# Attention inner loop on one Trainium2 core: one row-tiled stretch a step, and weighted sums over 512 columns one step behind

## What is computed

```python
scores = jnp.einsum('bqhd,bkhd->bhqk', Q, K) / np.sqrt(HEAD_DIM).astype(np.float32)
slopes = 0.5 ** jnp.arange(NUM_HEADS, dtype=jnp.float32)
rel = pos[None, :] - pos[:, None]
scores = scores + slopes[None, :, None, None] * rel[None, None, :, :]
attn = jax.nn.softmax(scores, axis=-1)
out = jnp.einsum('bhqk,bkhd->bqhd', attn, V)
```

## Time and profile before

| what | value |
|---|---|
| median of 3 runs | 5108.2 us (5095.89 to 5113.9) |
| span of the profiled execution | 5138.9 us (its own device time isn't listed) |
| TensorE busy / weight loads | 4706.1 us (92%) / 2589.8 us (50%) |
| VectorE, ScalarE busy | 4275.5 us (83%), 3471.8 us (68%) |
| GpSimd busy | 1377.0 us (27%) |
| mean granted TensorE clock | 0.936 |

### The profile page before, as it was taken

One profiled execution on the slowest core, in us unless ns is written; L12 is line 12 of the kernel. 1 busy time (PEld: TensorE's weight loads), 2 busy tenths in 40 slices (PEclk: granted clock), 3 DMA queues, 4 the chain that ended last, 5 costly groups with the idle time before them and its releaser, 6 DMA issues. The chain is left out here.

```text
span 5138.9 us, 109366 instructions
## 1 busy us (share of the span) xinstructions
PE 4706.1 (92%) x35413; PEld 2589.8 (50%) x35413; DVE 4275.5 (83%) x6882; ACT 3471.8 (68%) x6677; POOL 1377.0 (27%) x1279
## 2 busy tenths in 40 slices
PE   5869999999999999999999689999599999955998
PEld 4723333333333333333333267777366666645887
DVE  5779999999999999999999768878677877775554
ACT  2428888888888888888888523223377877734554
POOL 1111111111111111111111133333234443435776
PEclk8969999999999999999999889999699999956999
DMA  4931222212222122221222211111100000044442
GB/s 153 349 67 35 52 52 46 43 35 53 52 46 43 35 53 51 46 43 38 50 54 43 71 40 37 41 45 37 53 21 27 25 23 28 21 156 164 166 160 92
DMA packets 236717, 340.13 MB, mean 66 GB/s; under 512 B 60215, under 2 KB 170034, under 8 KB 227612
## 3 DMA queue, kind: packets, MB, share of 16 engines
q1 hardware_dynamic: 220032, 275.39, 22.3%
q0 software_dynamic: 16192, 58.43, 3.1%
HBM read 205.62 MB, written 136.18 MB: 67 GB/s over the span
## 5 line engine op out<-in xcount | busy, mean ns | idle before, releaser
L719 DVE TENSOR_REDUCE at_mxp<-at_ps_m 128x2 f32<-128x1024 f32 x2092 | 2524.4, 1221 | 70.2 <-PE at_ps_m L772 47.3
L692 ACT ACTIVATE at_prob<-at_ps_s 128x512 f32<-128x512 f32 x4100 | 2227.3, 596 | 323.5 <-PE at_ps_s L762 299.7
L782 PE MATMUL at_ps_o<-at_prob,at_vs 128*32 128x256 f32 x16384 | 1313.1, 392 | 13.9 <-ACT at_osum L698 13.9
L762 PE MATMUL at_ps_s<-at_qs,at_ks 51*128 51x512 f32 x4100 | 1036.7, 500 | 2.7 <-ACT at_prob L692 2.7
L772 PE MATMUL at_ps_m<-at_ks,at_qs 49*128 49x512 f32 x4184 | 859.0, 406 | 49.8 <-DMA at_ks<-t_alibi 34.4
L762 PEld LDWEIGHTS at_ps_s<-at_qs,at_ks 51*128 51x128 f32 x4100 | 384.6, 183 | 853.3 <-ACT at_prob L692 852.8
L782 PEld LDWEIGHTS at_ps_o<-at_prob,at_vs 128*32 128x32 f32 x16384 | 322.9, 108 | 778.2 <-issue 389.7
L564 POOL TENSOR_TENSOR at_total<-at_total,at_minus 128x16 f32<-128x16 f32 x65 | 189.6, 2917 | 1128.4 <-DMA at_total<-at_osum 1128.4
L772 PEld LDWEIGHTS at_ps_m<-at_ks,at_qs 49*128 49x128 f32 x4184 | 403.7, 190 | 73.7 <-DVE at_mxp L719 38.0
L67 DVE TENSOR_TENSOR ex_hidc<-ex_hid,ex_hidc 128x512 fp32r<-128x512 f32 x128 | 158.5, 1250 | 169.6 <-ACT ex_hid L2550 169.6
L1222 PE MATMUL mi_ps_f<-mi_w,mi_act 128*128 128x256 f32 x1024 | 260.1, 399 | 17.4 <-DVE mi_acc L1072 17.1
(11 more groups left out here) (317 smaller groups left out, 6161.6 us busy)
## 6 DMA issues: line engine op xcount, KB each, us to landing
t_parts<-pr_parts SPq DMA_DIRECT2D x64, 512.0 KB, 6.4
ex_w<-in_fw SPq DMA_DIRECT2D x32, 1024.0 KB, 7.4
at_ks<-t_parts SPq DMA_DIRECT2D x102, 256.0 KB
t_buf<-at_blank POOLq DMA_DIRECT2D x64, 384.5 KB, 3.2
at_qs<-t_parts SPq DMA_DIRECT2D x96, 256.0 KB
at_vs<-t_v SPq DMA_DIRECT2D x17, 1024.0 KB, 4.8
ex_rest<-t_buf SPq DMA_DIRECT2D x16, 1026.0 KB, 5.2
t_v<-pr_vaug SPq DMA_DIRECT2D x64, 256.0 KB, 5.6
```

What stands on the lines that cost most here:

```text
L692: nc.scalar.activation(prob[0 if up is None else (t + 1) % 2][:, j, :], ps_s[bank][:, :], ACT.Exp).then_inc(s_read, 1)
L719: nc.vector.tensor_reduce(out[:, s4, k + i, 2 * pair:2 * pair + 2], ps_m[i][:, :, :], AX.X, ALU.max).then_inc(mx_read, 1)
L762: nc.tensor.matmul(ps_s[bank][:, :], ks[s][a:a + QROWS, j // 2, t1 * P:(t1 + 1) * P], qs[s][a:a + QROWS, j // 2, c * T:(c + 1) * T], start ...
L782: last = nc.tensor.matmul(ps_o[32 * j:32 * j + 32, q0:q1], vs[s][:, t, 32 * j:32 * j + 32], prob[t % 2][:, j, q0:q1], start=(t == 0 and ha ...
```

## The change

The step is reordered. All row-tiled work stands together: scores 0 and 1, both maxima, scores 2 and 3. Then one weighted stretch over all 512 queries follows, and it takes the key tile of the step before. The scores of a step are now of heads 1, 2, 3 of its own key tile and head 0 of the next (`head`), so only one score is computed ahead of the loop. There are four `prob` buffers. The first step's weighted sums finish the chunk before, and ScalarE copies the sums after the first step's exponentials instead of before them; TensorE waits for the copy at the second step. A last weighted stretch stands behind the loop. At the very beginning the last `prob` buffer and a tile of `vs[1]` are set to ones, since the first weighted stretch reads them. The two halves of a maxima pair are issued in the order (1, 0), so that array halves still alternate. `RING` stays 3. The counts of `s_read` are shifted by `AHEAD` = 4 with an increment at the start.

```diff
--- before.py
+++ after.py
@@ -497,7 +497,8 @@
         qs = [sb(f"qs{s}", [P, HPG // 2, S], F32R) for s in range(2)]
         ks = [sb(f"ks{s}", [P, HPG // 2, S], F32R) for s in range(2)]
         vs = [sb(f"vs{s}", [P, KT, HPG * 32]) for s in range(2)]
-        prob = [sb(f"prob{r}", [P, HPG, T]) for r in range(2)]
+        PROBS = 4
+        prob = [sb(f"prob{r}", [P, HPG, T]) for r in range(PROBS)]
         mxp = [sb(f"mxp{r}", [P, SUB, MXS, HPG]) for r in range(2)]
         nmax = sb("nmax", [P, HPG, SUB])
         nparts = sb("nparts", [P, HPG, 2, SUB], F32R)
@@ -519,6 +520,7 @@
         turned, turned_out, sums_in, inverted = sem("turned"), sem("turned_out"), sem("sums_in"), sem("inverted")
         inverse_out, weight_in = sem("inverse_out"), sem("weight_in")
         norm_done, max_in, always, cleared = sem("norm_done"), sem("max_in"), sem("always"), sem("cleared")
+        before_first, sums_set = sem("before_first"), sem("sums_set")
         o_stored = [sem(f"o_stored{r}") for r in range(2)]
         TILES = SUB * HPG
         MXN = 2 * TILES
@@ -537,13 +539,20 @@
 
             return (k + (LOOP % RING == 1 and k >= LOOP // 2)) % RING
 
+        AHEAD = RING + 1
+        assert KT % PROBS == 0
+
         def place(up, n, t, j):
 
             k = (n * KT + t) * HPG + j
             if up is None:
-                return j, bank_of(LOOP - HPG + j), 0
+                return 0, bank_of(LOOP - 1), 0
             back = next(a for a in range(1, LOOP) if bank_of((k - a) % LOOP) == bank_of(k))
-            return HPG + up * LOOP + k, bank_of(k), back
+            return 1 + up * LOOP + k, bank_of(k), back
+
+        def head(t, j):
+
+            return (t, j + 1) if j < HPG - 1 else (t + 1, 0)
 
         def tile(t):
 
@@ -576,6 +585,8 @@
                 pool.drain()
                 nc.gpsimd.memset(qs[1][:, :, :].bitcast(F32), 1.0)
                 nc.gpsimd.memset(ks[1][:, :, :].bitcast(F32), 1.0).then_inc(ones_set[1], 1)
+                nc.gpsimd.memset(vs[1][:, KT - 1, :], 1.0)
+                nc.gpsimd.memset(prob[PROBS - 1][:, :, :], 1.0).then_inc(before_first, 1)
                 nc.gpsimd.memset(blank[:, :], 0.0)
                 pool.drain()
                 nc.gpsimd.memset(blank[:, 3 * D:ROW].bitcast(U32), 2 * N)
@@ -688,24 +699,26 @@
             def _(act):
                 def exponentials(up, n, t, j):
                     i, bank, _ = place(up, n, t, j)
+                    step, k = (0, 0) if up is None else head(t, j)
                     act.wait_ge(s_done, i + 1)
-                    nc.scalar.activation(prob[0 if up is None else (t + 1) % 2][:, j, :], ps_s[bank][:, :], ACT.Exp).then_inc(s_read, 1)
+                    nc.scalar.activation(prob[step % PROBS][:, k, :], ps_s[bank][:, :], ACT.Exp).then_inc(s_read, 1)
 
                 def take_sums(n):
 
                     act.wait_ge(norm_done, n)
-                    act.wait_ge(o_done, n)
+                    act.wait_ge(o_done, n + 1)
                     nc.scalar.copy(osum[:, :], ps_o[:, :]).then_inc(o_out, 1)
 
                 act.wait_ge(always, 1)
-                for j in range(HPG):
-                    exponentials(None, 0, 0, j)
+                act.sem_inc(s_read, AHEAD)
+                exponentials(None, 0, 0, 0)
                 with loop(nc, act, 0, TURNS) as up:
                     for r in range(CH):
-                        take_sums(up * CH + r)
                         for t in range(KT):
                             for j in range(HPG):
                                 exponentials(up, r, t, j)
+                            if t == 0:
+                                take_sums(up * CH + r)
                 take_sums(UNITS * QC)
 
             @block.vector
@@ -733,9 +746,7 @@
 
                 nc.vector.memset(qs[0][32:64, :, :].bitcast(F32), 1.0)
                 nc.vector.memset(ks[0][32:64, :, :].bitcast(F32), 1.0).then_inc(ones_set[0], 1)
-                nc.vector.memset(ps_o[:, :], 1.0)
-                dve.drain()
-                dve.sem_inc(always, 1)
+                nc.vector.memset(ps_o[:, :], 1.0).then_inc(sums_set, 1)
                 for t in range(LEAD):
                     if t == TILES:
                         negate(0)
@@ -755,12 +766,13 @@
             @block.tensor
             def _(pe):
                 def scores(up, n, t, j, s, c, t1):
-                    a = j % 2 * 64
+                    k = 0 if up is None else head(t, j)[1]
+                    a = k % 2 * 64
                     i, bank, back = place(up, n, t, j)
-                    if up is not None or j >= RING:
-                        pe.wait_ge(s_read, i - (back or RING) + 1)
-                    nc.tensor.matmul(ps_s[bank][:, :], ks[s][a:a + QROWS, j // 2, t1 * P:(t1 + 1) * P],
-                                     qs[s][a:a + QROWS, j // 2, c * T:(c + 1) * T], start=True, stop=True).then_inc(s_done, 1)
+                    if up is not None:
+                        pe.wait_ge(s_read, AHEAD + i - back + 1)
+                    nc.tensor.matmul(ps_s[bank][:, :], ks[s][a:a + QROWS, k // 2, t1 * P:(t1 + 1) * P],
+                                     qs[s][a:a + QROWS, k // 2, c * T:(c + 1) * T], start=True, stop=True).then_inc(s_done, 1)
 
                 def max_scores(n, s, c, t, i):
 
@@ -768,20 +780,18 @@
                     if not (isinstance(n, int) and n * MXN + 2 * t + i < 2):
                         pe.wait_ge(mx_read, n * MXN + 2 * t + i - 1)
                     q0 = c * T + s4 * P
-                    for a in range(2):
+                    for a in (1, 0):
                         last = nc.tensor.matmul(ps_m[i][:, a, :], qs[s][a * 64:a * 64 + MXR, pair, q0:q0 + P],
                                                 ks[s][a * 64:a * 64 + MXR, pair, (k + i) * T:(k + i + 1) * T], start=True, stop=True)
                     last.then_inc(mx_done, 1)
 
-                def weighted(up, r, s, t, half):
-
-                    q0, q1 = half * T // 2, (half + 1) * T // 2
-                    if half == 0:
-                        pe.wait_ge(s_read, HPG + up * LOOP + (r * KT + t) * HPG)
+                def weighted(up, r, s, t, steps):
+
+                    pe.wait_ge(s_read, AHEAD + 1 + up * LOOP + steps * HPG)
                     for j in range(HPG):
-                        last = nc.tensor.matmul(ps_o[32 * j:32 * j + 32, q0:q1], vs[s][:, t, 32 * j:32 * j + 32], prob[t % 2][:, j, q0:q1],
-                                                start=(t == 0 and half == 0), stop=(t == KT - 1), tile_position=(0, 32 * j), skip_group_check=True)
-                    if half and t + 1 == KT:
+                        last = nc.tensor.matmul(ps_o[32 * j:32 * j + 32, :], vs[s][:, t, 32 * j:32 * j + 32], prob[t % PROBS][:, j, :],
+                                                start=(t == 0), stop=(t == KT - 1), tile_position=(0, 32 * j), skip_group_check=True)
+                    if t + 1 == KT:
                         last.then_inc(o_done, 1)
 
                 pe.wait_ge(kq_in[0], 16 * NLD)
@@ -792,8 +802,9 @@
                     for i in range(2):
                         max_scores(0, 0, t // TILES, t, i)
                 pe.wait_ge(max_in, 16 * HPG)
-                for j in range(HPG):
-                    scores(None, 0, 0, j, 0, 0, 0)
+                pe.wait_ge(before_first, 1)
+                pe.wait_ge(sums_set, 1)
+                scores(None, 0, 0, 0, 0, 0, 0)
                 with loop(nc, pe, 0, TURNS) as up:
                     for r in range(CH):
                         uu, c = r // QC, r % QC
@@ -806,22 +817,22 @@
                             if (mc, t) == (QC, NEXT):
 
                                 pe.wait_ge(kq_in[1 - s], 16 * NLD * (up * (LU // 2) + (uu + 1) // 2 + 1))
+                            scores(up, r, t, 0, s, c, t)
+                            scores(up, r, t, 1, s, c, t)
+                            max_scores(*best, 0)
+                            max_scores(*best, 1)
+                            scores(up, r, t, 2, s, c, t)
                             if t + 1 == KT:
 
                                 pe.wait_ge(max_in, 16 * HPG * (n + 2))
-                            scores(up, r, t, 0, *nxt)
-                            scores(up, r, t, 1, *nxt)
-                            max_scores(*best, 0)
-                            if t == 0:
+                            scores(up, r, t, 3, *nxt)
+                            if t == 1:
 
                                 pe.wait_ge(o_out, n + 1)
                                 if c == 0:
                                     pe.wait_ge(v_in[s], 16 * (up * (LU // 2) + uu // 2 + 1))
-                            weighted(up, r, s, t, 0)
-                            scores(up, r, t, 2, *nxt)
-                            scores(up, r, t, 3, *nxt)
-                            max_scores(*best, 1)
-                            weighted(up, r, s, t, 1)
+                            weighted(up, r, s if t or c else 1 - s, (t - 1) % KT, r * KT + t)
```

(1 more changed line is left out.)

## The result

The changed kernel takes 5225.8 us (median of 4 runs, 5214.56 to 5235.58) against 5111.05 for the kernel before (5095.89 to 5132.02 in 4 runs): 1.0214 times as long, 95% interval 1.017 to 1.0258. The forecast was 5243, in a range of 5135 to 5310. The profiled execution has a span of 5234.0 us, where that of before had 5138.9.

The account below looks back on a forecast made before the run. TensorE's own sequence was taken to bound the kernel at 2.48 us a step. A chunk of 16 x 2.62 + 0.2 = 42.1 us against 40.00, over 64 chunks, gave +135 us: 5243 us, range 5135 to 5310.

Parts of the forecast that it names:

- The ring's chain: Attention loop: first score's load, its exponential, release, fourth score, wide weighted sums to next step; 2.62 us against 2.48.
- The lone fourth score: Fourth score's weight load to the weighted sums' load, after waiting for its bank: 0.43 us, between 0.33 and 0.67.
- Rival 1: The fourth score's weight load is hidden during its wait: 2.52 us a step, 5140 us; chance 6%.
- The maxima pair: Second maxima pair, awaiting the previous step's second reduction, loads 0.56 us into its step, hidden; at worst 0.1 us a chunk.
- Rival 2: Second maxima pair's wait for its reduction binds, not the score banks: 2.43 us a step, 5063 us, faster; chance 9%.
- The boundary: Between chunks: old idle at the sums' copy goes; the moved copy adds 0.2 us once a chunk.
- The total: Whole kernel: 64 chunks of 42.1 us against 40.00, +135 us, 5243 us on the median, 2.6% slower.
- The signs: Expected trace marks in the loop, among them ScalarE released by TensorE with some 0.65 us idle a step.
- rival 4: TensorE's granted clock falls in the loop because it waits each step: 5380 us or more; chance 4%.
- The maxima loop: Second maxima pair's load through next step's maxima and both reductions until its rewrite: 4.85 us for two steps, 2.43 each.

## Why the prediction was right, and by how much its terms were off

- **The ring's chain** was the term that mattered, and it held piece by piece: 0.54, 0.60, 0.05, 0.43 and 1.00 were forecast, and 0.53, 0.60, 0.05, 0.42 and 1.00 are in the rows. 2.62 against 2.605 us. It is shown from four sides: a bank more removes the wait, a bank less adds 0.49 us, a shorter exponential shortens the step, and moving what lies in between changes one step in sixteen, for a reason of its own.
- **The lone fourth score** was the only piece without a row, between 0.33 and 0.67. The 0.43 taken from a difference of two rows measured 0.42. Rival 1, by which its load would cost nothing, falls: from the load at 1502.77 to the sums at 1503.19 it is 0.42, not 0.33. The Trainium skill (TensorE: Matmul & The Clock Gate, Architectural detail: the array is 16× 32×32) says that a matmul can begin before its weights are all loaded. The 0.42 show nothing saved by it here.
- **The maxima pair** was said to wait until 0.56 into its step, hidden. It waited until 0.58, and the lighter reduction shows it hidden but for eight steps, each behind a negation. "Zero, at worst 0.1 us a chunk" was right: eight chunks lose 0.2 to 0.3, which is 0.03 a chunk on average.
- **Rival 2** was wrong as a forecast and right in its price: with a fourth bank two steps take 4.84 us, 2.42 each. The Trainium skill (TensorEngine Tiling, PSUM Bottleneck) warns that tiling speeds up TensorE and not the emptying of PSUM. The kernel with four banks agrees: TensorE waits there for VectorE's reduction (0.59 us idle at 1510.16). The change's own wait is of another kind, since ScalarE is idle for 0.55 us a step: a free bank is missing, not throughput.
- **The boundary** was mis-sized: 0.2 us a chunk was forecast, and 0.1 came. What was off is the copy's start, put at 0.84 + 0.43 = 1.27 us after the load of the weighted sums. It is 1.14 (1503.19 to 1504.33). The 0.84 had been read at a boundary where the copy came 0.48 after the exponential ahead of it, at ScalarE's own pace; the sums had ended by then (1507.34 and 0.64). Not every start that follows another is caused by it. So 0.1 too much here was within what had been allowed.
- **The total**: forecast +135 us, measured +115 by the medians. The difference is 64 x (42.1 - 41.8) = 19 us, 15 of them by the step's 0.015 and the others by the boundary. The step stands 1024 times in the kernel, so 0.01 us in reading a piece is 10 us. The signs were off in one place: 0.65 us idle a step was given for ScalarE, and 0.55 is in the rows, since four exponentials end 2.06 us after the first starts, not 1.97.
- **The clock** was 1.00 in the loop's stretch from 1000 to 1500 us, and rival 4 fell.

## What to carry over

Before work is gathered into one long stretch to save changes, follow each buffer of the ring around the new order: if a stretch holds more fills than there are buffers, the last one waits for a whole trip through the consumer (here 1.19 us), and what used to cover that trip now stands behind it. Alternating short stretches can cost switches and still be cheaper, because they interleave the trip with other work. And neither an engine that shows 99% busy nor a wait that shows in each step says what sets the time: a chain around the loop, closed piece by piece from starts in the timeline, does, and taking one wait away at a time tests it.

## What the runs showed of the hardware that I had not expected

- Sums of starts, read from the traces before and after, gave the steps of kernels that had a wait more or less: 2.43, 2.13 to 2.16 and 3.10 us were expected, and 2.42 (four banks), 2.13 to 2.19 (four banks, lighter reduction) and 3.10 (two banks) came. The half exponential was the exception: 256 columns took 0.38 us where 512 take 0.60.
- A reduction that follows another at once starts 1.13 to 1.14 us after it, though each is recorded with 1.21 to 1.22 us. Two such durations added up are 0.08 us longer than the 2.36 us that the pair takes from start to end.
- With a fourth bank the steps aren't even: from 1509.27 to 1511.81 it is 2.54 us, to 1514.11 it is 2.30. The maxima loop spans two steps, and away from the negation and the copy a longer one and a shorter one take turns in this trace.
